# Masked attention layers: maxima split by the upper halves of their words, and the projections' bank read between exponential and seed

## The chip, the cores and the metric

One core of a Trainium2 chip runs the whole network as one program. The metric is the device time of one execution in microseconds; the kernel before takes 3803.99 us (median of 3 runs, 3799.57 to 3808.73).

## The reference

Four transformer layers on x (8 batches x 512 rows x 256), each with cross attention (16 heads of depth 16, keys and values from a context of 512 rows) and a feed-forward part. Layers 0, 1 and 3 use masked attention; layer 1 also adds an adjacency matrix and masks with minus infinity, so that a row whose keys are all masked becomes NaN:

```python
scores = jnp.einsum('bhqd,bhkd->bhqk', Q, K) / jnp.sqrt(jnp.float32(D))
scores = scores + adj[None, None, :, :]                            # layer 1 only
scores = jnp.where(mask == 0, jnp.float32(-jnp.inf), scores)
weights = jax.nn.softmax(scores, axis=-1)
out = jnp.einsum('bhqk,bhkd->bhqd', weights, V)                    # then @ Wo + bo
```

Layer 2 (relative attention) and the four feed-forward parts are not touched.

## The kernel before, in words

Each layer part is a stage of its own, with a barrier of all engines behind it. The function `masked_attention` (L48) is called for layers 0, 1 and 3. A batch is 16 steps (4 groups of 4 heads, each with 4 blocks of 128 keys); a step has two half steps, called positions p = 0 to 31, each for two heads. Every engine runs its own list, in order, over these positions; semaphores tie them together. Batches 1 to 4 run in a loop of two rounds of two batches.

Scores are made twice. First the max units (`pe_max_unit`, L261): queries on partitions, 7 steps ahead; DVE adds the bias and reduces to the negated row maximum in one instruction (L460) into `nmax`. There are four max units to a step, two PSUM banks for them, and each unit waits until DVE has read the one two before it. Then the scores proper (`pe_scores`, L276), with keys on partitions, which need the maximum as three further rows of the contraction. Their bank `p2_ps[half]` is first filled with the turned bias: by ACT, the "seed" (`act_seed`, L512), or by two matmuls with the identity (L281). Function `by_act` decides: in layer 1 ACT seeds both half steps, in layers 0 and 3 only half 0. ACT takes the exponential of the bank (L529), and PE multiplies by the values (L292). ACT seeds the bank for step s+1 right behind the exponential of step s.

To bring the maxima into the contraction, DVE splits them at positions 2, 10, 18 and 26 (`dve_split_maxima`): copy to bf16 (L405), remainder (L408), copy to bf16 (L411), remainder (L414), each waiting for the one before, and placed between and behind the position's two reductions. The last one raises `m_split`. At the next position (3, 11, 19, 27) PE turns the parts into rows (`pe_maxima`, L251) in the shared bank `front_ps`, ACT copies these to `m_row` (L490), and SP issues four DMAs into the query stack. In layer 1 the split at position 26 is joined by `dve_all_masked`, three DVE instructions (L420, L422, L424) that make the NaN rows from `nmax`.

The bank `front_ps` is shared by all side work of a batch: values at positions 0 and 4, the output projection at 8 and 12 (both read by DVE), turned input at 14 and 16, key projection at 20 and 22, query projection at 24 and 28 (read by ACT in `act_shared`, L484 and L497), and the four maxima. PE makes a projection in two pieces around the position's second max unit; it waits for the read of the bank's use before. ACT reads the bank at the start of the position behind, so behind the seed. POOL (`pool_frame`) splits queries and keys, makes the mask biases, and adds the output bias to the residual in one instruction (L546).

Of the kernel before, what the change touches and what calls it, by code (L numbers as in the profile page):

```python
# [14 lines left out]
P = 128  # L15
# [32 lines left out]
def masked_attention(nc, x_sb, ident, ident_bf, ctxT_dram, w, layer, mask, maskT, adj=None, adjT=None):  # L48
# [15 lines left out]
    with ctx:  # L64
        def sb(name, shape, dt):
            return ctx.enter_context(nc.sbuf_tensor(f + name, shape, dt))
# [26 lines left out]
        heads_out = sb("heads_out", [P, S], F32)  # L93
        heads_outT = sb("heads_outT", [P, DC, S], F32)
        rsum = sb("rsum", [P, BLOCKS, 1], F32)
        nmax = sb("nmax", [P, 2, TPB, GH], F32)
        m_rest = sb("m_rest", [P, TPB, GH], F32)
        m_parts = sb("m_parts", [P, TPB, GH, 3], BF16)
        m_row = sb("m_row", [GH * 3, 2, S], BF16)
        ones_row = sb("ones_row", [3, S], BF16)  # L100
        stats = sb("stats", [P, TPB, 6], F32)
# [145 lines left out]
        def pe_maxima(pe, n, j, base, b):  # L247
            pe.wait_ge(front_read, base + n)
            pe.wait_ge(m_split, b * NG + j + 1)
            for t in range(TPB):  # L250
                last = nc.tensor.matmul(front_ps[0:GH * 3, t * P:(t + 1) * P],  # L251
                                        m_parts[:, t, :, :].rearrange("p h k -> p (h k)"), ident_bf[:, :],
                                        start=True, stop=True)
            last.then_inc(front_full, 1)

# [138 lines left out]
                nc.vector.tensor_tensor(tiles, front_ps[:, :].rearrange("p (a n) -> p a n", a=2), tiles,  # L394
                                        ALU.add).then_inc(front_read, 1)

        def dve_split_maxima(dve, b, j, step):

            G = b * NG + j
            if step == 0:  # L400
                dve.wait_ge(maxed, (G + 1) * GH * TPB)
                if later(G):

                    dve.wait_ge(m_row_ready, G)
                nc.vector.tensor_copy(m_parts[:, :, :, 0], nmax[:, j % 2, :, :]).then_inc(m_step, 1)  # L405
            elif step == 1:
                dve.wait_ge(m_step, G * 3 + 1)
                nc.vector.tensor_tensor(m_rest[:, :, :], nmax[:, j % 2, :, :], m_parts[:, :, :, 0], ALU.subtract).then_inc(m_step, 1)  # L408
            elif step == 2:
                dve.wait_ge(m_step, G * 3 + 2)  # L410
                nc.vector.tensor_copy(m_parts[:, :, :, 1], m_rest[:, :, :]).then_inc(m_step, 1)  # L411
            else:
                dve.wait_ge(m_step, G * 3 + 3)
                nc.vector.tensor_tensor(m_parts[:, :, :, 2], m_rest[:, :, :], m_parts[:, :, :, 1], ALU.subtract).then_inc(m_split, 1)  # L414

        def dve_all_masked(dve, b, par):

            k = b * 3
            nan = nan_rows[:, par, :]
            nc.vector.tensor_scalar(nan, nmax[:, 0, :, 0], 1e29, 3e38, ALU.is_gt, ALU.mult).then_inc(nan_step, 1)  # L420
            dve.wait_ge(nan_step, k + 1)
            nc.vector.tensor_scalar(nan, nan, 3e38, 0.0, ALU.mult, ALU.mult).then_inc(nan_step, 1)  # L422
            dve.wait_ge(nan_step, k + 2)
            nc.vector.tensor_scalar(nan, nan, 0.0, None, ALU.add).then_inc(nan_step, 1)  # L424

        def dve_split_first(dve, which, i):

# [10 lines left out]
        def dve_positions(dve, b, par, positions, plan):  # L438
            for p in positions:
                s, half = p // 2, p % 2  # L440
                pair = (2 * half, 2 * half + 1)
                split = group_split(b, p)
                a, over, j, t = ahead(s)
                for n, kind, i in shared(plan, p, 1):
                    dve_shared(dve, n, kind, i, uses_before(b), b, par)
                if split is not None:
                    dve_split_maxima(dve, b, split, 0)
                if has(b, a) and half == 0:
                    if every_mask and j == 0:
                        dve.wait_ge(bias_ready, (b + over) * MK + t + 1)  # L450
                    G = b * NG + a // TPB
                    if t == 0 and later(G - 1):
                        dve.wait_ge(m_split, G - 1)
                for i in pair:
                    if has(b, a):
                        unit = (b * STEPS + a) * GH + i
                        if later(unit - NX + 1):
                            dve.wait_ge(maxed, unit - NX + 1)
                        dve.wait_ge(p1_done, unit + 1).then_inc(apart_dve, 1)
                        nc.vector.tensor_tensor_reduce(  # L460
                            out=sums[:, i % NX, :], in0=p1_ps[i % 2][:, :], in1=bias[:, t, :],
                            scale=-1.0, scalar=3.4028235e38, op0=ALU.add, op1=ALU.min,
                            accum_out=nmax[:, a // TPB % 2, t, i:i + 1]).then_inc(maxed, 1)
                    if split is not None:
                        if i == pair[0] and adj is not None and split % NG == 0:
                            dve_all_masked(dve, b + split // NG, (par + split // NG) % 2)
                        dve_split_maxima(dve, b, split, i % 2 + 1)
                if split is not None:
                    dve_split_maxima(dve, b, split, 3)
                j = (p - HEADS) // 8  # L470
                if (p - HEADS) % 8 < 4 and has(b, j * TPB):
                    dve_heads(dve, b, j, (p - HEADS) % 8)
                if has(b + 2, 0) and p == 7 and not opening(b):
                    dve_norm_input(dve, b + 2)
                if has(b + 2, 0) and p == 9:
                    dve_apply_norm(dve, b + 2)
# [37 lines left out]
        def act_positions(act, b, par, positions, plan):  # L514
            for p in positions:
                s, half = p // 2, p % 2
                for n, kind, i in shared(plan, p, 1):
                    act_shared(act, n, kind, i, uses_before(b), b, par)
                if p % 8 == 2 and has(b, s - 2):
                    G = b * NG + (s - 2) // TPB  # L520
                    act.wait_ge(pv_done, (G + 1) * TPB * GH)
                    if later(G):
                        act.wait_ge(o_turned, G)
                    nc.scalar.activation(oT_sb[:, :], oT_ps[:, :], ACT.Copy).then_inc(oT_read, 1)
                if has(b, s):
                    if later(b * STEPS + s - 1):
                        act.wait_ge(pv_done, (b * STEPS + s - 1) * GH)
                    act.wait_ge(p2_done, b * HALVES + p + 1).then_inc(apart_act, 1)
                    nc.scalar.activation(probs[:, s % 2 * 2 + half, :, :], p2_ps[half][:, :, :], ACT.Exp).then_inc(exp_done, 1)  # L529
                over, t = (s + 1) // STEPS, (s + 1) % STEPS  # L530
                if has(b, s + 1) and by_act(t, half):
                    act_seed(act, b, over, t, half)
# [8 lines left out]

        def pool_residual(pool, bn):
            pool.wait_ge(xn_ready, bn + 1)
            tile = x_sb[:, bass.ds(bn * TPB, TPB), :]
            bo = bo_bc[:, :].rearrange("p (a n) -> p a n", a=1).to_broadcast([P, TPB, D])
            nc.gpsimd.tensor_tensor(tile, tile, bo, ALU.add).then_inc(residual_biased, 1)  # L546

        def pool_split(pool, bn, which, i):

# [31 lines left out]
        def pool_frame(pool, b, par):  # L581

            after, then = has(b, 0) and has(b + 1, 0), has(b + 2, 0)
            for s in range(STEPS):
                if s == 0 and every_mask and has(b, 0) and later(b):
                    pool_mask(pool, b, MK - 1)
                if s in (1, 2) and after:
                    pool_split(pool, b + 1, 0, s - 1)
                if s == 3 and has(b + 1, 0):
                    pool_residual(pool, b + 1)  # L590
                if s == 4 and then and not opening(b):
                    pool_norm(pool, b + 2)
# [2323 lines left out]
```

## Time and profile before

| what | value |
|---|---|
| median of 3 runs | 3803.99 us |
| profiled execution, its span | 3814.43 us, 3812.7 us |
| masked layer 0, layer 1, layer 3 (start to next stage's start) | 16.1 to 672.2, 942.6 to 1673.1, 2754.0 to 3403.2 us |
| mean granted TensorE clock | 0.91 |
| PE, DVE, ACT, POOL busy share | 83%, 66%, 59%, 29% |

The stage starts are those of each stage's first POOL instruction. The three masked layers take 656.1, 730.5 and 649.2 us, together 2035.8 us, over half of the span. The busy share of an engine is a mean over stages with different limits. In rows of the timeline the first column is the start, the second the duration; in brackets stands the engine's idle time ahead of the instruction and who ended it. A matmul's duration is modelled and overlaps the next one's.

### The profile page before, as it was taken

What the parts mean: (1) busy time and instruction counts of PE and PEld (TensorE: products, weight loads), DVE (VectorE), ACT (ScalarE), POOL (GpSimd) and SP (SyncE); (2) the same over time, 40 slices, a digit from 0 to 9 for tenths busy, and PEclk for the clock granted to TensorE, in tenths of its full rate; (3) what the DMA queues carried; (4) which work ended last, traced back from release to release, by engine and by line L of the source; (5) the groups of instructions that cost most, each with busy time, mean ns of one, the idle gap of its engine ahead of it and who ended that gap; (6) DMA issues with size and microseconds to landing.
All of it is one profiled execution on the core that took longest, in us unless ns stands there. A gap on an engine that the chain in (4) does not pass through costs nothing. (4 is left out here: it accounts for less than half of the span.)

```text
span 3812.7 us, 67413 instructions
## 1 busy us (share of the span) xinstructions
PE 3150.8 (83%) x17142; PEld 1603.2 (42%) x17249; DVE 2502.5 (66%) x7668; ACT 2250.3 (59%) x3026; POOL 1117.3 (29%) x1194
## 2 busy tenths in 40 slices
PE   5999998787788888849977888888279999965997
PEld 3343432343333333216644555555134344324565
DVE  4777776787676677743225777878867787755431
ACT  1777777664388888951116666676547777750111
POOL 4344441000454555201114333331332221100332
PEclk8999999898799899969988999999589999985899
DMA  5322320000433334110028999997031221102332
GB/s 147 87 71 69 96 72 13 23 0 31 123 96 95 84 95 112 51 52 1 0 55 291 293 289 292 296 321 257 24 82 41 58 63 40 35 29 94 77 101 67
DMA packets 212155, 392.88 MB, mean 103 GB/s; under 512 B 24633, under 2 KB 76985, under 8 KB 211657
## 3 DMA queue, kind: packets, MB, share of 16 engines
q1 hardware_dynamic: 168777, 296.38, 28.1%
q10 hardware_dynamic: 36864, 83.90, 5.9%
q0 software_dynamic: 6144, 8.39, 1.3%
q8 instruction: 143, 2.34, 0.3%
q14 instruction: 227, 1.86, 0.2%
HBM read 189.88 MB, written 96.47 MB: 75 GB/s over the span
## 5 line engine op out<-in xcount | busy, mean ns | idle before, releaser
L460 DVE CUSTOM_DVE_ANT_0 A_sums<-A_p_ps,A_bias 128x512 bf16<-128x512 f32 x1536 | 1039.3, 688 | 434.0 <-PE A_p_ps L261 392.7
L529 ACT ACTIVATE A_probs<-A_p_ps 128x1024 f32<-128x1024 f32 x768 | 780.6, 1018 | 281.3 <-PE A_p_ps L276 186.2
L261 PE MATMUL A_p_ps<-A_k_stack,A_q_stack 96*128 96x512 bf16 x1536 | 604.0, 396 | 116.4 <-DVE A_nmax L460 109.8
L512 ACT ACTIVATE A_p_ps<-A_biasT 128x1024 f32<-128x1024 bf16 (+1 forms) x512 | 526.1, 1028 | 62.1 <-ACT A_probs L529 2.4
L276 PE MATMUL A_p_ps<-A_q_stack,A_k_stack 99*128 99x512 bf16 x1536 | 471.5, 389 | 39.0 <-ACT A_p_ps L512 34.4
L292 PE MATMUL A_oT_ps<-A_probs,A_v_aug 128*17 128x512 f32 x3072 | 419.1, 618 | 0.7 <-ACT A_probs L529 0.7
L261 PEld LDWEIGHTS A_p_ps<-A_k_stack,A_q_stack 96*128 96x128 bf16 x1536 | 149.7, 97 | 630.5 <-DVE A_nmax L460 539.7
L1100 DVE CUSTOM_DVE_ANT_0 A_scores<-A_qk_ps,A_rel_in 128x384 f32<-128x384 f32 (+3 forms) x512 | 232.5, 486 | 84.3 <-PE A_qk_ps L984 76.3
L1007 PE MATMUL A_t_ps<-ident,A_scores 128*128 128x128 f32 x1280 | 227.7, 299 | 61.4 <-DVE A_probsT L1090 52.6
L1155 ACT ACTIVATE A_rel_out<-A_rel_ps 128x1024 f32<-128x1024 f32 (+3 forms) x256 | 179.9, 703 | 144.0 <-PE A_rel_ps L973 142.4
L1090 DVE COPY A_probsT<-A_t_ps 128x384 f32<-128x384 f32 (+3 forms) x512 | 229.1, 485 | 54.1 <-PE A_t_ps L1007 46.4
L1162 ACT ACTIVATE A_scores<-A_scores,A_nmax 128x384 f32<-128x384 f32 (+3 forms) x512 | 257.4, 555 | 7.3 <-DVE A_nmax L1100 7.2
L276 PEld LDWEIGHTS A_p_ps<-A_q_stack,A_k_stack 99*128 99x128 bf16 x1536 | 144.1, 100 | 180.5 <-ACT A_p_ps L512 73.3
L1182 POOL TENSOR_SCALAR_AFFINE_SELECT A_rel_in<-A_rel_in 128x256 f32<-128x256 f32 x256 | 102.6, 409 | 397.3 <-DMA A_rel_in<-A_rel_dram 393.4
L1007 PEld LDWEIGHTS A_t_ps<-ident,A_scores 128*128 128x128 f32 x1280 | 151.8, 149 | 138.1 <-issue 56.4
L574 POOL TENSOR_SCALAR A_bias<-A_mask_in 128x512 bf16<-128x512 int32 (+2 forms) x68 | 131.5, 1934 | 209.0 <-DVE A_nmax L460 187.9
L574 POOL TENSOR_SCALAR A_biasT<-A_mask_in 128x512 bf16<-128x512 int32 (+2 forms) x68 | 131.9, 1940 | 136.9 <-PE A_p_ps L281 70.3
L2786 ACT ACTIVATE M_hid<-M_h_ps,M_b 128x512 f32<-128x512 f32 x64 | 44.0, 687 | 189.2 <-PE M_h_ps L2588 186.7
L555 POOL CAST A_parts<-A_qk 128x512 bf16<-128x512 f32 x84 | 51.2, 609 | 334.6 <-ACT A_qk L497 334.2
L2105 ACT ACTIVATE U_hid<-U_h_ps,U_hid_bias 128x512 f32<-128x512 f32 x64 | 44.0, 687 | 176.0 <-PE U_h_ps L1943 175.9
L984 PE MATMUL A_qk_ps<-A_k_stack,A_q_stack 96*128 96x384 bf16 (+3 forms) x512 | 127.2, 313 | 12.6 <-DVE A_nmax L1100 11.1
L281 PE MATMUL A_p_ps<-A_biasT,ident_bf 128*128 128x512 bf16 x420 | 132.6, 379 | 5.2
(345 smaller groups left out, 5452.2 us busy)
## 6 DMA issues: line engine op xcount, KB each, us to landing
A_k_stack<-A_parts SPq DMA_DIRECT2D x192, 256.0 KB, 5.0
A_q_stack<-A_parts SPq DMA_DIRECT2D x192, 256.0 KB, 5.5
A_rel_dram<-A_rel_out ACTq DMA_DIRECT2D x64, 512.0 KB, 5.0
A_rel_in<-A_rel_dram SPq DMA_DIRECT2D x64, 512.0 KB, 5.7
A_rel_dram<-A_rel_out ACTq DMA_DIRECT2D x64, 384.0 KB, 4.8
A_rel_in<-A_rel_dram SPq DMA_DIRECT2D x64, 384.0 KB, 5.3
A_ctxT<-in_ctxT SPq DMA_DIRECT2D x32, 512.0 KB, 6.4
A_mask_in<-in_mask SPq DMA_DIRECT2D x64, 256.0 KB, 4.5
```

The source lines that it names most:

```text
L261: nc.tensor.matmul(p1_ps[i % 2][:, :], q_stack[0:KS, a_par, j * GH + i, t * P:(t + 1) * P], k_stack[0:KS, a_par, j * GH + i, :], start=Tru ...
L276: last = nc.tensor.matmul(p2_ps[half][:, i % 2, :], k_stack[:, par, j * GH + i, kb * P:(kb + 1) * P], q_stack[:, par, j * GH + i, :], star ...
L292: nc.tensor.matmul(oT_ps[CW * i:CW * i + HD + 1, :], v_aug[:, v_par, kb, j * GH + i, :], probs[:, (s - 1) % 2 * 2 + i // 2, i % 2, :], sta ...
L460: nc.vector.tensor_tensor_reduce(out=sums[:, i % NX, :], in0=p1_ps[i % 2][:, :], in1=bias[:, t, :], scale=-1.0, scalar=3.4028235e38, op0=A ...
L512: nc.scalar.activation(p2_ps[half][:, :, :], turned, ACT.Copy).then_inc(seeded, 1)
L529: nc.scalar.activation(probs[:, s % 2 * 2 + half, :, :], p2_ps[half][:, :, :], ACT.Exp).then_inc(exp_done, 1)
L574: last = nc.gpsimd.tensor_scalar(dst, mask_in[:, k % 2, :], 0.0, NEG, ALU.is_equal, ALU.mult)
L1007: last = nc.tensor.transpose(t_ps[:, i, kb, :], scores[(p - TURN_LAG) % NP][:, i, kb * P:(kb + 1) * P], ident[:, :])
L1090: nc.vector.tensor_copy(probsT[u % NP][:, i, 0:nk, :], t_ps[:, i, 0:nk, :]).then_inc(copied, 1)
L1100: nc.vector.tensor_tensor_reduce(out=scores[p % NP][:, i, 0:n], in0=qk_ps[i][:, 0:n], in1=rel_in[s % NI][:, (2 * half + i) * n:(2 * half + ...
L1155: nc.scalar.activation(rel_out[a % NO][:, 2 * half * n:(2 * half + 2) * n].rearrange("p (i n) -> p i n", i=2), rel_ps[:, :, 0:n], ACT.Copy ...
L1162: nc.scalar.activation(scores[u % NP][:, i, 0:n], scores[u % NP][:, i, 0:n], ACT.Exp, bias=nmax[:, u % NP, i:i + 1], scale=-1.0).then_inc( ...
```

## The change

The maxima lie in a new tile `maxima` [P, 2, TPB, 3, GH] of f32. The reduction writes part 0. The bf16 part that PE uses is not a copy but the upper half of each f32 word, seen through a bitcast with a stride of two; two subtractions on DVE make the parts 1 and 2. The maxima's rows in `m_row` are ordered part by part, so that SP's four DMAs read partitions with a stride of 4. DVE's guard for a new group waits for `m_row_ready` in place of `m_split`. The NaN rows are made by POOL at step 14. POOL's residual bias is four instructions of 128x256 in place of one of 128x1024. ACT reads the shared bank in the same position: behind its exponential and ahead of its seed.

```diff
-        nmax = sb("nmax", [P, 2, TPB, GH], F32)
-        m_rest = sb("m_rest", [P, TPB, GH], F32)
-        m_parts = sb("m_parts", [P, TPB, GH, 3], BF16)
+        maxima = sb("maxima", [P, 2, TPB, 3, GH], F32)
+        maxima_high = maxima[:, :, :, :, :].rearrange("p a t k h -> p (a t k h)").bitcast(BF16)[:, 1::2].rearrange(
+            "p (a t k h) -> p a t k h", a=2, t=TPB, k=3)
...
-        def dve_split_maxima(dve, b, j, step):
+        def dve_split_maxima(dve, b, j, k):
...
+            whole, high = maxima[:, j % 2, :, k, :], maxima_high[:, j % 2, :, k, :]
+            if k == 0:
                 dve.wait_ge(maxed, (G + 1) * GH * TPB)
...
+                dve.wait_ge(m_step, G + 1)
+            nc.vector.tensor_tensor(maxima[:, j % 2, :, k + 1, :], whole, high,
+                                    ALU.subtract).then_inc((m_step, m_split)[k], 1)
...
                     if t == 0 and later(G - 1):
-                        dve.wait_ge(m_split, G - 1)
+                        dve.wait_ge(m_row_ready, G - 1)
+                    if t == 0 and adj is not None and a // TPB % NG == 2:
+                        dve.wait_ge(nan_step, (b + over) * 3 + 1)
...
-                    if split is not None:
-                        if i == pair[0] and adj is not None and split % NG == 0:
-                            dve_all_masked(dve, b + split // NG, (par + split // NG) % 2)
-                        dve_split_maxima(dve, b, split, i % 2 + 1)
-                if split is not None:
-                    dve_split_maxima(dve, b, split, 3)
+                    if split is not None and i == pair[0]:
+                        dve_split_maxima(dve, b, split, 1)
...
         def act_positions(act, b, par, positions, plan):
             for p in positions:
                 s, half = p // 2, p % 2
-                for n, kind, i in shared(plan, p, 1):
-                    act_shared(act, n, kind, i, uses_before(b), b, par)
...
                     nc.scalar.activation(probs[:, s % 2 * 2 + half, :, :], p2_ps[half][:, :, :], ACT.Exp).then_inc(exp_done, 1)
+                for n, kind, i in shared(plan, p):
+                    act_shared(act, n, kind, i, uses_before(b), b, par)
                 over, t = (s + 1) // STEPS, (s + 1) % STEPS
                 if has(b, s + 1) and by_act(t, half):
                     act_seed(act, b, over, t, half)
...
+            for t in range(TPB):
+                tile = x_sb[:, bass.ds(bn * TPB + t, 1), :].rearrange("p a n -> p (a n)")
+                last = nc.gpsimd.tensor_tensor(tile, tile, bo_bc[:, :], ALU.add)
+            last.then_inc(residual_biased, 1)
+
+        def pool_all_masked(pool, bn, par):
+
+            k, nan = bn * 3, nan_rows[:, par, :]
+            pool.wait_ge(m_split, bn * NG + 1).then_inc(apart_pool, 1)
+            if later(bn - 1):
+                pool.wait_ge(front_read, use_of(bn - 1, "out", 1) + 1).then_inc(apart_pool, 1)
+            nc.gpsimd.tensor_scalar(nan, maxima[:, 0, :, 0, 0], 1e29, 3e38, ALU.is_gt, ALU.mult).then_inc(nan_step, 1)
...
+                if s == 14 and adj is not None and has(b + 1, 0):
+                    pool_all_masked(pool, b + 1, 1 - par)
...
-                             m_row[3 * h:3 * h + 3, j % 2, :]).then_inc(m_placed[j % 2], 16)
+                             m_row[h:GH * 3:GH, j % 2, :]).then_inc(m_placed[j % 2], 16)
```

## Rows read from the trace of the kernel before

**Rows 1.** Page, costliest groups: ACT's exponentials and seeds.
```profile
L529 ACT ACTIVATE A_probs<-A_p_ps 128x1024 f32<-128x1024 f32 x768 | 780.6, 1018 | 281.3 <-PE A_p_ps L276 186.2
L512 ACT ACTIVATE A_p_ps<-A_biasT 128x1024 f32<-128x1024 bf16 (+1 forms) x512 | 526.1, 1028 | 62.1 <-ACT A_probs L529 2.4
```

**Rows 2.** Busy (count) of PE, PEld, DVE, ACT, POOL by window; clock; DMA; GB/s.
```profile
1416.93:1499.38 82.45, 69.89 (x345) 28.69 (x345) 59.99 (x182) 71.31 (x80) 43.43 (x36) 0.94 0.36 97
396.00:470.00 74.00, 69.68 (x370) 30.08 (x375) 56.96 (x177) 55.78 (x63) 33.10 (x27) 1.00 0.32 80
```

**Rows 3.** Idle before L251 in layer 1, by releaser: us, times.
```profile
  DVE A_m_parts L414: 51.3, 34
```

**Rows 4.** Waits in layer 1: us in total, times, longest.
```profile
PE A_front_ps L230 <- ACT A_m_row L490: 8.1, 6, 2.1
```

**Rows 5.** ACT's waits in layer 1 from 1043.5 to 1661 us.
```profile
ACT A_probs L529 <- PE A_p_ps L276: 31.5, 44, 2.7
ACT A_qk L497 <- PE A_front_ps L230: 7.4, 8, 1.6
```

**Rows 6.** Timeline of DVE, layer 1, a split at position 26.
```profile
1416.79 1.23 DVE L420 TENSOR_SCALAR A_nan_rows<-A_nmax 128x4 f32<-128x4 f32 x1
...
1418.26 0.52 DVE L424 TENSOR_SCALAR A_nan_rows<-A_nan_rows 128x4 f32<-128x4 f32 x1
...
1420.14 0.19 DVE L414 TENSOR_TENSOR A_m_parts<-A_m_rest,A_m_parts 128x16 bf16<-128x16 f32 x1
```

**Rows 7.** Timeline of POOL at that time.
```profile
1416.73 1.26 POOL L578 TENSOR_TENSOR A_biasT<-A_biasT,A_adj_in 128x512 f32<-128x512 f32 x1
```

**Rows 8.** Timeline of PE at that time.
```profile
1420.38 0.39 PE L251 MATMUL A_front_ps<-ident_bf,A_m_parts 128*12 128x128 bf16 x4 [2.63 <-DVE A_m_parts L414]
```

**Rows 9.** Timeline of ACT behind that split.
```profile
1423.60 1.02 ACT L529 ACTIVATE A_probs<-A_p_ps 128x1024 f32<-128x1024 f32 x1 [1.44 <-PE A_p_ps L276]
...
1426.56 0.69 ACT L497 ACTIVATE A_qk<-A_front_ps,A_bq 128x512 f32<-128x512 f32 x1 [0.79 <-PE A_front_ps L230]
```

**Rows 10.** Timeline of ACT behind a split at position 2, layer 1.
```profile
1278.49 1.02 ACT L529 ACTIVATE A_probs<-A_p_ps 128x1024 f32<-128x1024 f32 x1 [1.94 <-PE A_p_ps L276]
```

**Rows 11.** Another of the same, and a key read at position 20.
```profile
1487.02 0.69 ACT L497 ACTIVATE A_qk<-A_front_ps,A_bk 128x512 f32<-128x512 f32 x1 [1.60 <-PE A_front_ps L230]
...
1527.86 1.02 ACT L529 ACTIVATE A_probs<-A_p_ps 128x1024 f32<-128x1024 f32 x1 [0.65 <-PE A_p_ps L276]
```

**Rows 12.** Timeline of PE and ACT, layer 1, key projection at position 22.
```profile
1408.07 1.03 PE L230 MATMUL A_front_ps<-A_ctxT,A_wk 128*128 128x256 f32 x4
...
1407.43 1.01 ACT L529 ACTIVATE A_probs<-A_p_ps 128x1024 f32<-128x1024 f32 x1
...
1409.51 0.67 ACT L497 ACTIVATE A_qk<-A_front_ps,A_bk 128x512 f32<-128x512 f32 x1
```

**Rows 13.** Timeline of PE and ACT, layer 0, key projection at position 20.
```profile
431.77 1.03 PE L230 MATMUL A_front_ps<-A_ctxT,A_wk 128*128 128x256 f32 x4
...
435.24 0.60 PE L276 MATMUL A_p_ps<-A_q_stack,A_k_stack 99*128 99x512 bf16 x2
...
430.97 1.02 ACT L529 ACTIVATE A_probs<-A_p_ps 128x1024 f32<-128x1024 f32 x1 [0.59 <-PE A_p_ps L276]
...
433.08 0.67 ACT L497 ACTIVATE A_qk<-A_front_ps,A_bk 128x512 f32<-128x512 f32 x1
```

**Rows 14.** Idle before L251 by releaser, in layer 0 and then in layer 3.
```profile
  DVE A_m_parts L414: 10.9, 22
...
  DVE A_m_parts L414: 12.4, 23
```

**Rows 15.** Timeline of all engines, layer 1, a split beside POOL's residual.
```profile
1271.55 2.35 POOL L546 TENSOR_TENSOR x_sb<-x_sb,A_bo_bc 128x1024 f32 x1
1271.66 2.28 DVE L414 TENSOR_TENSOR A_m_parts<-A_m_rest,A_m_parts 128x16 bf16<-128x16 f32 x1
```

**Rows 16.** Line L405: duration in ns, shortest, median, longest.
```profile
L405 DVE CAST A_m_parts<-A_nmax x96: 174/183/2035, 69.3 to 3369.8; 128x16 bf16<-128x16 f32 x96
```

More of the change, by code:

```diff
@@ L251, in pe_maxima @@
                 last = nc.tensor.matmul(front_ps[0:GH * 3, t * P:(t + 1) * P],
-                                        m_parts[:, t, :, :].rearrange("p h k -> p (h k)"), ident_bf[:, :],
+                                        maxima_high[:, j % 2, t, :, :].rearrange("p k h -> p (k h)"), ident_bf[:, :],
                                         start=True, stop=True)
@@ L395, in dve_shared @@
                                         ALU.add).then_inc(front_read, 1)
-        def dve_split_maxima(dve, b, j, step):
+        def dve_split_maxima(dve, b, j, k):
             G = b * NG + j
-            if step == 0:
+            whole, high = maxima[:, j % 2, :, k, :], maxima_high[:, j % 2, :, k, :]
+            if k == 0:
                 dve.wait_ge(maxed, (G + 1) * GH * TPB)
[L402 to L411, printed above, removed]
-            else:
[L413 to L424, printed above, removed]
+            else:
+                dve.wait_ge(m_step, G + 1)
+            nc.vector.tensor_tensor(maxima[:, j % 2, :, k + 1, :], whole, high,
+                                    ALU.subtract).then_inc((m_step, m_split)[k], 1)
         def dve_split_first(dve, which, i):
@@ L462, in dve_positions @@
                             scale=-1.0, scalar=3.4028235e38, op0=ALU.add, op1=ALU.min,
-                            accum_out=nmax[:, a // TPB % 2, t, i:i + 1]).then_inc(maxed, 1)
-                    if split is not None:
-                        if i == pair[0] and adj is not None and split % NG == 0:
-                            dve_all_masked(dve, b + split // NG, (par + split // NG) % 2)
-                        dve_split_maxima(dve, b, split, i % 2 + 1)
-                if split is not None:
-                    dve_split_maxima(dve, b, split, 3)
+                            accum_out=maxima[:, a // TPB % 2, t, 0, i:i + 1]).then_inc(maxed, 1)
+                    if split is not None and i == pair[0]:
+                        dve_split_maxima(dve, b, split, 1)
                 j = (p - HEADS) // 8
@@ L543, in pool_residual @@
             pool.wait_ge(xn_ready, bn + 1)
-            tile = x_sb[:, bass.ds(bn * TPB, TPB), :]
-            bo = bo_bc[:, :].rearrange("p (a n) -> p a n", a=1).to_broadcast([P, TPB, D])
-            nc.gpsimd.tensor_tensor(tile, tile, bo, ALU.add).then_inc(residual_biased, 1)
+            for t in range(TPB):
[8 more added lines that the diff above has]
+            nc.gpsimd.tensor_scalar(nan, maxima[:, 0, :, 0, 0], 1e29, 3e38, ALU.is_gt, ALU.mult).then_inc(nan_step, 1)
+            pool.wait_ge(nan_step, k + 1).then_inc(apart_pool, 1)
+            nc.gpsimd.tensor_scalar(nan, nan, 3e38, 0.0, ALU.mult, ALU.mult).then_inc(nan_step, 1)
+            pool.wait_ge(nan_step, k + 2).then_inc(apart_pool, 1)
+            nc.gpsimd.tensor_scalar(nan, nan, 0.0, None, ALU.add).then_inc(nan_step, 1)
         def pool_split(pool, bn, which, i):
```

## The prediction

> **What bounds the kernel now.** I read the page's costliest groups first, then one batch of each masked layer by window, then the waits, then the timeline around the splits. The reader is to see two different limits.
>
> In layers 0 and 3 it is PE. A batch takes 74.0 us, and PE is busy for 69.7 of them; ACT has 55.8, DVE 57.0 [rows 2]. What PE loses there is lost for good; what ACT or DVE gain is not seen.
>
> In layer 1 ACT seeds both half steps. Exponentials and seeds take 1018 and 1028 ns each [rows 1]; back to back a pair takes some 2.1 us, so 32 pairs make 67 of a batch's 82.5 us. With the bank reads and the copies of the outputs (some 0.5 us each, fourteen) ACT is at about 75. Its busy share by window, 71.3 of 82.5 us, is the union of overlapping rows; PE has 69.9 [rows 2]. So ACT is the bound, and time is lost where ACT itself stands: 31.5 us for scores and 7.4 us for a projection from 1043.5 to 1661 us [rows 5], 38.9 in all. PE's own waits matter only as far as they come back as such idle time.
>
> **The split of the maxima.** Before: four DVE instructions of about 0.18 us in a group, and the last comes behind the position's second reduction. After: two, the second behind the first reduction. Some 0.36 us of DVE work goes, and `m_split` comes earlier by that and by one reduction (0.69 us or a little less). What counts is PE at L251. In layer 1 it stood for the last remainder (L414) 51.3 us in 34 waits [rows 3]. These are of two kinds.
>
> At position 26 the NaN rows are made between the two reductions. L420 starts at 1416.79 and L424 ends at 1418.78, so 1.99 us; the split ends at 1420.33 [rows 6]. PE had stood 2.63 us when its transposes began [rows 8], so it was ready at 1417.75. ACT then stood 1.44 us before an exponential and 0.79 before the projection behind it [rows 9], 2.23 us in all. Without the NaN work and the two last instructions the second subtraction would start at about 1416.8, where L420 did. But POOL has an instruction from 1416.73 to 1417.99 [rows 7], and L420 took 1.23 us on four elements a partition, to just POOL's end. The same is seen where L414 took 2.28 us beside POOL's 2.35 us residual and ended with it [rows 15]. I take the subtraction to be held likewise, to 1418.2: PE still stands 0.4 us, and 1.8 us of ACT's 2.23 come back. The split comes eight times; I count six (in the others ACT doesn't stand behind it): 11 us.
>
> The Trainium skill, "GPSIMD Engine Reference", section Key points, says that GpSimd shares its SBUF interfaces with VectorE and contends with instructions in a two-port mode or with two SBUF inputs. That speaks against this change, as both instructions left have two SBUF inputs; the trace agrees for L414. By that rule the saving at position 26 is 1.8 us, as taken; without it, 2.2.
>
> At position 2 ACT stood 1.94 us behind the split beside the residual [rows 10], and 0.65 us in a common case [rows 11]. There are six such, from 0.5 to 2.5 us with what follows. The residual in four pieces of a quarter (2.35/4, so 0.6 us) holds DVE for at most 0.6 us instead of 2.28. One us each: 6 us.
>
> In layers 0 and 3 the idle ahead of L251 for L414 is 10.9 and 12.4 us [rows 14]. This counts the weight loads' queue too, which stands without harm while matmuls run, so half is an upper guess: 5 us each, which takes in one copy in layer 0 that POOL held for 2.04 us [rows 16]. Together 10; the bounds are 0 and 23.3.
>
> **The read of the bank, maxima.** Layer 1 only (half 1 has no seed in layers 0 and 3, so nothing changes there). The read goes ahead of a seed of 1.03 us. PE stood 8.1 us for it before the key and query projections [rows 4]; ACT paid with waits such as 1.60 us before a key read [rows 11]. Of ACT's 7.4 us [rows 5] some 4 don't follow a NaN split; I take 3. The seed behind it is later by the read, 0.6 us, and PE then has a projection to do first, so nobody waits. Bounds 0 and 4.4.
>
> **The read of the bank, projections.** This is the cost. Before, ACT seeded while PE finished the projection; now ACT stands behind its exponential until the bank is full. In layer 1 the exponential ends at 1408.44 and the projection at 1409.10 [rows 12]: 0.66 us. But a delayed ACT finds PE further ahead at the next read, so in a run of three reads it is paid once: 0.7 us in each of six batches with projections, 4.2 us. Turned input (positions 14, 16) is short and ready in time. In layer 0 the exponential ends at 431.99, the projection at 432.80 [rows 13]: ACT stands 0.81 us. The read (issued 0.15 later, 0.6 long) and the seed (1.03) then end at about 434.6; PE's scores that need the seed start at 435.24 [rows 13]. Cover of 0.6 us, so nothing is lost; if it were gone, each read would cost up to 0.81.
>
> **The rest.** DVE's guard on `m_row_ready` is for the group before the last, long read: 0. POOL's three tiny instructions (the fastest such row on DVE is 0.17 us; POOL, some 0.3 each) sit between bias builds; DVE needs the first only three steps later, and ACT's seeds need the mask build behind it over 5 us later: 0, at most 1 us a batch. SP issues the same four DMAs per group, of three rows each, and the scores need them four positions later: 0. PE's weights with a stride of two: 12 columns, 0; bounds 0 to 0.1 us for each of 96 groups. Strided operands on DVE, 16 elements: the same, either sign.
>
> **Sum.** Layer 1: 11 + 6 + 3 - 4.2, about 16 us. Layers 0 and 3: 10. Together 26 us less. The profiled execution took 3814.4 us around its span of 3812.7, so 3788; it lies 10.4 above the median of 3804.0, so the median becomes 3778.
>
> **Rivals.**
> A, larger: ACT's waits in layer 1 go altogether (38.9 us) and the full 23.3 of layers 0 and 3 return: 62 us less, 3742. For it: ACT is the bound and all its releasers are PE. Against: the largest waits near position 10 stem from DVE's norm, which stays.
> B, hidden: PE's waits vanish and come back as waits for seeds or for POOL-held subtractions, so the change doesn't bring `m_split` forward where it matters. Left are the NaN instructions and little else, about 5 us: 3799. For it: two-input instructions are held by POOL [rows 7, 15], and the reads make seeds later.
> C, slower: the stand between exponential and seed. It decides from the point where PE's next scores already wait for the seed, a cover of 0.6 us in layers 0 and 3. Price: 24 reads in each, 48 x 0.81 = 39 us, and 24 x 0.66 = 16 in layer 1, less the 26 + 4 gained elsewhere: 25 slower, 3829. For it: the seeds are late by 1.5 us in every such position. Against: ACT stands idle for 18 of 74 us there.
>
> **How the numbers follow.** About 0.2%, 8 us, is what a measurement of this kernel can tell from no change. Forecast 0.56 (own range 3760 to 3792), A 0.12, B 0.20, C 0.12. B lies at the edge, so a quarter of it counts as faster: faster 0.73, same 0.15, slower 0.12. For eight in ten I go from 3748, near A, to 3803, past B; C is left out.
>
> **What would show it.** Right: in layer 1, L251's idle for the split falls from 51 to under 15 us; a batch takes 80 us instead of 82.5; ACT's rows show a stand of 0.3 to 0.8 us before L497 directly behind an exponential; POOL's residual rows are 0.6 us. In layers 0 and 3 a batch takes 73.3 to 74 us, and L276 doesn't wait for L512 more than now. Wrong: PE's scores in layers 0 and 3 wait for seeds behind every key or query read; the two subtractions are often over 1 us; layer 1's batch stays at 82 us though L251 no longer waits.

## The result

The changed kernel takes 3746.17 us (median of 4 runs, 3740.91 to 3750.79) against 3806.36 us of the kernel before in the same runs: ratio 0.9842, interval 0.9818 to 0.9865, 60 us less. Run once more, beside other runs of the kernel before, it came to 0.9859 (0.9841 to 0.9877). The prediction was 3778, 26 us less, where 60 came. The measured time lies 2 us below the low end of the range (3748).

The title names the bank reads of the projections only. The change moves all of ACT's bank reads between exponential and seed, the maxima's too, and that one turns out to be the part that pays.

The profiled execution has a span of 3744.7 us. By stage, from the first POOL instruction of each:

| stage, us | before | after | predicted difference |
|---|---|---|---|
| masked layer 0 | 656.1 | 647.8 | -5 |
| masked layer 1 | 730.5 | 686.3 | -16 |
| masked layer 3 | 649.2 | 645.2 | -5 |
| the five untouched stages | 1760.8 | 1749.4 | 0 |

The untouched stages differ by 11 us with the same code; over all kernels of this study layer 2's attention took between 707 and 717 us, whatever was changed. So a single profile's stages carry some 5 us of scatter each. The two profiles differ by 68 us (that of the kernel before is of an execution 8 us above the median), the medians by 60. A quieter measure is used below: in layer 1 the time from the first copy of the outputs' bank (L524 before, L502 after) to the 29th, 28 groups or seven batches. In the changed kernel these are the two rows (timeline of ACT; start, duration):

```profile
1021.89 0.58 ACT L502 ACTIVATE A_oT_sb<-A_oT_ps 128x512 f32<-128x512 f32 x1
...
1554.20 0.58 ACT L502 ACTIVATE A_oT_sb<-A_oT_ps 128x512 f32<-128x512 f32 x1
```

So 532.3 us; before it was 568.4 (from 1043.49 to 1611.92). That is 36 of the layer's 44 us. The second profile of the changed kernel gave 528.8. Layers 0 and 3 over the same 28 groups: 512.7 to 505.7 and 510.5 to 507.0.

The page's groups that answer to [rows 1], ACT's exponentials and seeds (busy, mean ns, idle before):

```profile
L507 ACT ACTIVATE A_probs<-A_p_ps 128x1024 f32<-128x1024 f32 x768 | 780.4, 1017 | 220.6 <-PE A_p_ps L276 148.2
L492 ACT ACTIVATE A_p_ps<-A_biasT 128x1024 f32<-128x1024 bf16 (+1 forms) x512 | 525.8, 1027 | 52.3 <-ACT A_m_row L470 7.5
```

The work is the same, the exponentials' idle time fell by 61 us. One batch by window, columns as in [rows 2]:

```profile
1360.00:1435.00 75.00, 66.31 (x344) 26.26 (x342) 55.46 (x168) 69.47 (x78) 43.90 (x41) 0.98 0.39 106
380.00:453.00 73.00, 69.41 (x375) 29.88 (x374) 55.01 (x167) 54.92 (x62) 33.20 (x30) 1.00 0.31 79
```

In these windows layer 1's batch went from 82.5 to 75 us (mean of the seven batches: 81.2 to 76.0) and ACT is busy for 69.5 of them, 93%. PE does the same work in 66.3 instead of 69.9 us, at a granted clock of 0.98 instead of 0.94 of full speed. Over the whole 28 groups, before and after:

```profile
1043.49:1611.92 568.43, 476.60 (x2345) 184.91 (x2345) 414.03 (x1241) 495.29 (x542) 283.94 (x224) 0.94 0.33 89
1021.89:1554.20 532.31, 462.04 (x2344) 176.86 (x2344) 388.02 (x1161) 487.82 (x542) 291.11 (x263) 0.97 0.35 95
```

In these stretches the granted clock is either 1.00 or 0.50 of full speed. From the means 0.94 and 0.97 some 70 us at half speed can be worked out before and some 30 after, and PE is busy 14.6 us less with the same work. One such stretch of before: PE stood 2.63 us at L251 until 1420.38 [rows 8], and from 1421.90 to 1425.30 the granted clock is 0.50. PE's shorter time can be a part of why ACT waits less for it; how large a part, no run separates. What L251 waits for in layer 1, as in [rows 3]:

```profile
  issue: 13.4, 29
  DVE A_maxima L405: 1.3, 3
```

51.3 us became 1.3 (of the 51.3, 28.1 stood on PE's matmul queue and 23.2 on the weight loads'). [rows 5] cover a longer stretch than 28 groups, so here are ACT's waits over the 28 groups alone, before:

```profile
ACT A_probs L529 <- PE A_p_ps L276: 30.2, 41, 2.7
ACT A_qk L497 <- PE A_front_ps L230: 7.4, 8, 1.6
ACT A_probs L529 <- issue: 3.8, 1, 3.8
ACT A_probs L529 <- ACT A_m_row L490: 3.7, 12, 0.4
```

and after:

```profile
ACT A_probs L507 <- PE A_p_ps L276: 15.2, 19, 3.6
ACT A_p_ps L492 <- ACT A_m_row L470: 6.9, 28, 0.3
ACT A_qk L477 <- PE A_front_ps L230: 1.7, 8, 0.3
```

Of 37.6 us for PE 16.9 are left. With the waits that name another releaser or none (one wait of 3.6 to 3.8 us is given to PE in one profile and to "issue" in another) the idle time in rows fell by 22 us, of a gain of 36. The other 14 are not idle time in any row. They are in the distances between ACT's instructions. Before, with the maxima read behind the seed (timeline of ACT, kernel before):

```profile
1419.50 1.01 ACT L529 ACTIVATE A_probs<-A_p_ps 128x1024 f32<-128x1024 f32 x1
1420.62 1.03 ACT L512 ACTIVATE A_p_ps<-A_biasT 128x1024 f32<-128x1024 f32 x1
1421.59 0.57 ACT L490 ACTIVATE A_m_row<-A_front_ps 12x512 bf16<-12x512 f32 x1
```

and after:

```profile
1373.38 1.01 ACT L507 ACTIVATE A_probs<-A_p_ps 128x1024 f32<-128x1024 f32 x1
1374.29 0.57 ACT L470 ACTIVATE A_m_row<-A_front_ps 12x512 bf16<-12x512 f32 x1
1375.14 1.03 ACT L492 ACTIVATE A_p_ps<-A_biasT 128x1024 f32<-128x1024 f32 x1 [0.28 <-ACT A_m_row L470]
1376.10 1.01 ACT L507 ACTIVATE A_probs<-A_p_ps 128x1024 f32<-128x1024 f32 x1
1377.27 0.69 ACT L477 ACTIVATE A_qk<-A_front_ps,A_bq 128x512 f32<-128x512 f32 x1 [0.17 <-PE A_front_ps L230]
1377.86 1.02 ACT L492 ACTIVATE A_p_ps<-A_biasT 128x1024 f32<-128x1024 f32 x1
```

The seed starts 1.12 us behind its exponential, since it overwrites the bank and waits for that one's end. The bank read doesn't wait: it starts 0.91 behind. So a read in this place costs 0.22 us less than behind the seed. From the exponential to the next one, in steps with a read of the maxima, it took 3.05 us before (median, with 0.22 or 0.39 of wait for the read's own end) and takes 2.72 after. With turned input it is 2.58 and 2.33, with a projection 2.70 and 2.58. The 28 groups hold 28, 12 and 24 such steps: by these medians 9, 3 and 3 us, together some 15. This distance from start to start is called the pitch below.

### The profile page after: what moved, and what is told of

The parts are those of the page before. It is cut to its first block and busy times, and to the rows that moved or that the text cites. A ratio compares the mean times of both kernels' runs of the same rounds, so it can differ in the third digit from the quotient of the medians.

```text
span 3744.7 us, 67361 instructions
## 1 busy us (share of the span) xinstructions
PE 3126.9 (84%) x17249; PEld 1590.8 (42%) x17249; DVE 2445.0 (65%) x7452; ACT 2234.1 (60%) x3026; POOL 1133.9 (30%) x1290
## 5 line engine op out<-in xcount | busy, mean ns | idle before, releaser
L276 PEld LDWEIGHTS A_p_ps<-A_q_stack,A_k_stack 99*128 99x128 bf16 x1536 | 141.4, 99 | 183.9 <-ACT A_p_ps L492 81.2
L281 PE MATMUL A_p_ps<-A_biasT,ident_bf 128*128 128x512 bf16 x512 | 152.6, 378 | 0.0
```

Source lines behind the costliest of these rows:

```text
L276: last = nc.tensor.matmul(p2_ps[half][:, i % 2, :], k_stack[:, par, j * GH + i, kb * P:(kb + 1) * P], q_stack[:, par, j * GH + i, :], star ...
```

## The experiments

All times are medians against runs of the kernel before on the same chip. "28 groups" is the stretch of layer 1 told above, one profiled execution each; two of the changed kernel differ by 3.5 us, so only differences well over that are read. "Early" means between exponential and seed, "late" behind the seed.

| kernel | median us | ratio, interval | 28 groups us |
|---|---|---|---|
| before | 3804 to 3812 | 1 | 568.4 |
| changed | 3746.17; 3753.81 | 0.9842 (0.9818, 0.9865); 0.9859 (0.9841, 0.9877) | 532.3; 528.8 |
| changed, all reads late | 3791.92 | 0.9953 (0.9936, 0.9970) | 561.3 |
| before, all reads early | 3790.03 | 0.9955 (0.9937, 0.9973) | 550.3 |
| before, NaN rows on POOL | 3809.97 | 1.0006 (0.9989, 1.0023) | 564.1 |
| before, new split | 3798.28 | 0.9972 (0.9955, 0.9989) | 571.9 |
| changed, only maxima early | 3763.04 | 0.9888 (0.9866, 0.9911) | 531.8 |
| changed, only projections early | 3791.47 | 0.9955 (0.9942, 0.9968) | 567.1 |
| changed, outputs' copy early too | 3745.56 | 0.9823 (0.9800, 0.9846) | 524.2 |
| changed, NaN rows on DVE | 3749.28 | 0.9863 (0.9837, 0.9890) | 531.2 |
| before, split and maxima early | 3766.13 | 0.9882 (0.9863, 0.9901) | 539.4 |
| before, maxima early | 3788.07 | 0.9944 (0.9924, 0.9965) | 551.9 |
| changed, filler ahead of each seed | 3755.49 | 0.9863 (0.9847, 0.9879) | 530.7 |
| changed, residual in one piece | 3753.52 | 0.9852 (0.9832, 0.9873) | 532.2 |
| changed, outputs early, row signal late | 3744.16 | 0.9829 (0.9810, 0.9847) | 523.2 |

**Each part by itself.** First the reads put back in the changed kernel:

```diff
             for p in positions:
                 s, half = p // 2, p % 2
+                for n, kind, i in shared(plan, p, 1):
+                    act_shared(act, n, kind, i, uses_before(b), b, par)
...
-                for n, kind, i in shared(plan, p):
-                    act_shared(act, n, kind, i, uses_before(b), b, par)
                 over, t = (s + 1) // STEPS, (s + 1) % STEPS
```

> The changed kernel with one part undone: ACT reads the shared bank again at the start of the next position, behind the seed. Theory 1 (order): in the trace of after a seed starts 1.13 us behind its exponential, since it waits for that exponential's end, while a bank read starts 0.91 behind it and the seed 0.48 (input, 0.59 projection) behind the read; so a read in between costs 0.22 us less, 36 such in layer 1, and for the maxima 2.72 against 3.05 us, 30 such: 16 to 18 us in layer 1, so this kernel takes about 3764 us and its layer 1 some 703 us instead of 686. Theory 2 (the prediction's): the reads ahead of the seed cost ACT 4 us, the maxima's read gives 3, so this kernel stays at 3746 plus or minus 3.

Measured 3791.92, far slower than either theory said: all other parts together are worth 7 us of the 36 in 28 groups, and 0.5% in all. The prediction's count for the reads (3 gained, 4 lost) is refuted. Then the same edit the other way round, on the kernel before:

> The kernel before with this one part of the change: ACT reads the shared bank between exponential and seed. Theory 1 (order): layer 1 gains 16 us or a little more, 3788 us; layers 0 and 3 nothing. Theory 2 (the prediction's): gain 3, cost 4, so 3806 plus or minus 3. Rival C of the prediction: slower, up to 3829, with PE's scores waiting for seeds in layers 0 and 3.

3790.03 and 18 us in 28 groups, as the pitch would have it; layer 0's stage took 656.1 us as before and 28 groups of layers 0 and 3 took 512.7 and 509.6 us against 512.7 and 510.5, so rival C is refuted too. But 18 and 7 make 25, not 36.

The NaN rows alone:

```diff
-                        if i == pair[0] and adj is not None and split % NG == 0:
-                            dve_all_masked(dve, b + split // NG, (par + split // NG) % 2)
...
+                if s == 14 and adj is not None and has(b + 1, 0):
+                    pool_all_masked(pool, b + 1, 1 - par)
```

> The kernel before with this one part: the NaN rows are made by POOL at step 14. Prediction's way of counting: ACT's idle behind the split at position 26 is 2.2 us in each of six batches, most of it from the NaN work of 1.99 us, so 10 us less, 3796. If PE's wait of 2.6 us comes back in full in all eight batches: 18 us less, 3788. Layers 0 and 3 unchanged.

Nothing that the medians show, and 4 us in 28 groups, which is within the scatter. PE's stand at position 26, 1.3 to 2.6 us in the eight splits before, fell to 0.5 to 1.3 us, but that was not worth the 11 us of the sum. And the split alone (with the new order of the rows in `m_row` and DVE's guard, which belong to it):

```diff
-                nc.vector.tensor_copy(m_parts[:, :, :, 0], nmax[:, j % 2, :, :]).then_inc(m_step, 1)
...
+            nc.vector.tensor_tensor(maxima[:, j % 2, :, k + 1, :], whole, high,
+                                    ALU.subtract).then_inc((m_step, m_split)[k], 1)
```

> The kernel before with this one part: the maxima split by the upper halves of their words, two subtractions, NaN rows still on DVE, reads late, residual in one piece. Prediction's way: layers 0 and 3 gain 4 to 5 us each, layer 1 some 6: 3791. If only the stands seen on PE's matmul queue count (2.6 and 3.8 us in layers 0 and 3): 3794. In layer 1 the idle of L251 for the split falls by the two last instructions and one reduction, about 1 us at positions 2 and 26.

9 us less in all, and none of it in layer 1's 28 groups (571.9). PE's waits from 929 us to the end of layer 1 show where it went (us in total, times, longest):

```profile
PE A_front_ps L230 <- ACT A_m_row L480: 13.5, 11, 2.1
PE A_front_ps L235 <- ACT A_m_row L480: 10.4, 6, 2.0
PE A_front_ps L251 <- DVE A_maxima L405: 8.0, 7, 1.2
PE A_front_ps L242 <- ACT A_m_row L480: 3.6, 2, 2.0
```

At L251 PE stands 8 us instead of 28.1 on its matmul queue, and 27.5 us instead of 14.5 (8.1 at L230, 3.4 at L235, 3.0 at L242) for ACT's read of the maxima before the next projection. Much of the stand has moved one step on.

**Which reads.** Only the maxima's read early, with the rest of the change:

```diff
+                for n, kind, i in shared(plan, p, 1):
+                    if not (kind == "m"):
+                        act_shared(act, n, kind, i, uses_before(b), b, par)
...
                 for n, kind, i in shared(plan, p):
-                    act_shared(act, n, kind, i, uses_before(b), b, par)
+                    if (kind == "m"):
+                        act_shared(act, n, kind, i, uses_before(b), b, par)
```

> The changed kernel, but only the maxima's read stays between exponential and seed; the six reads of projections and turned input per batch go back behind the seed. So far in layer 1, over 28 groups in the middle of the layer: before 568.5 us, reads early alone 550.2, all but the reads 561.3, the whole change 532.3. So 11 us come only when both are there. Theory I (maxima chain): an early m_split is worth nothing while the maxima's read stands behind a seed of 1 us, and PE's next projection waits for that read; then this kernel keeps the interaction and loses only the pitch of 36 reads x 0.22 = 8 us less the 5 us ACT stands for the bank: about 3750. Theory II (ACT is just full): the interaction comes from ACT's shorter work as such, whichever reads; then half of all is lost: about 3765.

28 groups 531.8, all of the gain. The reads of projections and turned input are worth nothing there that can be seen; that their pitch and ACT's stand for the bank cancel is the likely reading. The median is 17 us above the changed kernel's first one and 9 above its second; whether a few us of that are real is not settled. The reverse, with the condition turned round:

> The reverse: projections and turned input are read between exponential and seed, the maxima's read goes back behind the seed. Theory I (maxima chain): the interaction of 11 us goes, and 30 x 0.33 = 10 us of pitch, so about 21 to 30 us over the changed kernel: 3770 to 3776. Theory II: about half of the reads' part, 3760.

567.1, close to the 568.4 of the kernel before: without the maxima's read all the rest of the change is worth 1 us in layer 1, and 7 where the projections' reads are late too (561.3). So with the maxima late, the projections' early reads cost some 6 us, in one profile each. PE's waits in it from 929 us to the end of layer 1:

```profile
PE A_front_ps L230 <- ACT A_m_row L470: 22.6, 12, 2.1
PE A_front_ps L235 <- ACT A_m_row L470: 11.0, 6, 2.0
PE A_front_ps L242 <- ACT A_m_row L470: 3.2, 2, 1.6
```

36.8 us, against these in the changed kernel (929 to 1616 us; L242's row there is under 1):

```profile
PE A_front_ps L230 <- ACT A_m_row L470: 9.8, 12, 0.9
PE A_front_ps L235 <- ACT A_m_row L470: 3.9, 6, 0.8
```

With `m_split` early the read is ready to go, but it stands in ACT's list behind a seed of 1 us; PE's next projection waits for it, and ACT's read of that projection, or the scores behind it, then wait for PE. ACT's largest waits in this kernel, over its 28 groups, show the way back:

```profile
ACT A_probs L510 <- PE A_p_ps L276: 23.9, 32, 2.4
ACT A_qk L477 <- PE A_front_ps L230: 19.1, 13, 2.8
```

43.0 us for PE, where the changed kernel has 16.9. It is a loop through both engines.

**Does it need the NaN rows on POOL?** In the changed kernel they go back to DVE, between the two reductions:

```diff
                     if split is not None and i == pair[0]:
+                        if adj is not None and split % NG == 0:
+                            dve_all_masked(dve, b + split // NG, (par + split // NG) % 2)
                         dve_split_maxima(dve, b, split, 1)
```

> The changed kernel with the NaN rows back on DVE, between the two reductions at position 26. Alone on the kernel before, moving them gave nothing that the medians show (1.0006 [0.9989, 1.0023]) and 4.5 us in 28 groups of layer 1. Theory I (maxima chain): with the read early the 2 us of DVE work are now on the chain eight times: 12 to 16 us over the changed kernel, 3760. Rival: ACT's or DVE's slack hides it here too: 3746 to 3750.

531.2 and 3749: the rival, they are hidden here too. Next the smallest pair, on the kernel before: the new split and the maxima's read, nothing else (the two edits shown above).

> The kernel before with two parts only: the split by upper halves, and the maxima's read (alone) between exponential and seed. NaN rows on DVE, residual in one piece, projections read late. Chain theory: these two are the whole gain; 28 groups of layer 1 take 532 us plus or minus 4, layers 0 and 3 as in the changed kernel, so 3750 to 3760. Rival: what is missing (NaN rows on POOL, residual in pieces) works only together; then 545 us or more and over 3770.

Between the two: 539.4, that is 29 of the 36 us. And the maxima's read without the split:

> The kernel before with one part: the maxima's read between exponential and seed, the old split of four instructions. Chain theory: the read early shortens the chain by a seed, the late split (25 us of stand at L251 in 28 groups) stays: between 568 and 532, about 550 us as with all reads early, 3788. Rival: the read alone does it all, 532 to 538.

551.9: 16 us by itself, at an unchanged granted clock (0.94 over the 28 groups, as before), so this part of the gain doesn't come through the clock. So over 28 groups the split is worth -3 (slower, within the scatter) with the read late, and 12 with it early.

**The changed kernel again,** as the reference on that chip:

> The changed kernel itself once more, on the chip of the next three, as their reference. Expected at its first ratio, 0.984, so some 60 us under the kernel before, with 532 us over 28 groups of layer 1. If the kernel with only the maxima read early (0.9888 in the last call, yet 531.8 us over the same groups) is really slower, this one must be clearly below 0.989; if that was the scatter between executions, the two meet.

0.9859, clearly below 0.9888 only by the middle values; the intervals (0.9841 to 0.9877, 0.9866 to 0.9911) touch. So it stays open as said.

**The residual in one piece,** for the 8 us between 539.4 and 531.8:

```diff
+            tile = x_sb[:, bass.ds(bn * TPB, TPB), :]
+            bo = bo_bc[:, :].rearrange("p (a n) -> p a n", a=1).to_broadcast([P, TPB, D])
+            nc.gpsimd.tensor_tensor(tile, tile, bo, ALU.add).then_inc(residual_biased, 1)
```

> The changed kernel with POOL's residual back in one instruction of 2.35 us. Between the kernel with split and maxima's read alone (539.4 us over 28 groups of layer 1) and the one with the NaN rows on POOL and the residual in four pieces (531.8) lie 8 us, and the NaN rows back on DVE changed nothing (531.2). Residual theory: this kernel takes 537 to 540 us there, and a DVE instruction of the split is again seen with 1 us or more beside the residual; 3758. Rival: NaN rows and residual cover for each other, either alone is enough; then 532 and 3750.

532.2: no effect in layer 1. In layer 0 one batch of seven took 80.6 us instead of 77.5, the one where a split meets the residual. So neither the NaN rows nor the residual, taken back singly, costs the 8 us. Both together do seem to: with the projections' reads late, the kernel that has both takes 531.8 us and the one that has neither 539.4; with all reads late it is 561.3 and 571.9. That they cover for each other fits this, but no run takes back exactly these two from the changed kernel.

**The pitch by itself.** An instruction without use ahead of every seed of layer 1:

```diff
         def act_seed(act, b, over, s, half):
+            if adj is not None:
+                n = seeds(b + over, s, half)
...
+                    act.wait_ge(filled, n - 1).then_inc(apart_act, 1)
+                    nc.scalar.activation(filler[:, :], bq_sb[:, 0:1], ACT.Copy).then_inc(filled, 1)
```

> The changed kernel with an extra instruction on ACT, 128 x 1 elements, ahead of every seed of layer 1 (256 in all). It does nothing for the result. Pitch theory: where no read stands there, ACT is idle 0.22 us until the exponential has ended, so the filler fits in: seed still 1.13 us behind the exponential, 190 fillers free, and only the 66 behind a read cost some 0.1 to 0.2 us each: 532 us become 540 at most, 3755. Rival: the 0.22 us are ACT's own cost to turn from one instruction to the next; then each filler adds its 0.2 us, 45 us in 28 groups, 3795.

530.7 and 3755.49 beside 528.8 and 3753.81 of the changed kernel on the same chip, where 224 fillers of 0.20 us in the 28 groups would be 45 us. 160 of them stand directly behind an exponential, and there they cost nothing. The 28 behind the maxima's read do lengthen their step, from 2.72 to 2.92 us (medians), some 6 us in all; in the total that doesn't show. In its timeline the seed still starts 1.13 us behind the exponential, with the filler in between:

```profile
1179.65 1.02 ACT L516 ACTIVATE A_probs<-A_p_ps 128x1024 f32<-128x1024 f32 x1
1180.55 0.20 ACT L488 ACTIVATE A_filler<-A_bq 128x1 f32<-128x1 f32 x1
1180.78 1.03 ACT L501 ACTIVATE A_p_ps<-A_biasT 128x1024 f32<-128x1024 f32 x1
```

So the 0.22 us are a real gap, which other work fills, and not ACT's own cost of turning from one instruction to the next.

**Going on in that direction.** The copy of the outputs' bank put into the same gap, in layer 1:

```diff
-                if p % 8 == 2 and has(b, s - 2):
...
+                if adj is not None:
+                    act_outputs(act, b, s, p)
                 for n, kind, i in shared(plan, p):
                     act_shared(act, n, kind, i, uses_before(b), b, par)
```

> The changed kernel, and in layer 1 the copy of the outputs' bank (once in a group, at the first half of its second step) also goes between exponential and seed. Theory of the pitch: a seed starts 1.13 us behind its exponential because it waits for that one's end, anything else 0.91 behind it, so each copy saves 0.22 us: 31 x 0.22 = 6.8 us where ACT is the bound, so 3740. Rival: the copy comes a microsecond later, PE's first product of the next group waits for it, and the time stays at 3746 or rises by up to 10.

524.2: 8 us less than the first profile of the changed kernel and 4.6 less than the second, 6.8 expected. The step with the copy takes 2.33 instead of 2.57 us (median of 27), so the pitch is as expected. The ratio, 0.9823, can't be told from the changed kernel's. Then the signal for the maxima's rows behind the seed as well:

```diff
                 if has(b, s + 1) and by_act(t, half):
                     act_seed(act, b, over, t, half)
+                for n, kind, i in shared(plan, p):
+                    if kind == "m" and adj is not None:
+                        act.wait_ge(front_read, uses_before(b) + n + 1).then_inc(m_row_ready, 1)
```

> The changed kernel with two more moves on ACT in layer 1: the outputs' copy between exponential and seed (measured before: 524.2 against 532.3 and 528.8 us over 28 groups), and the wait for the maxima's read, which raises m_row_ready, put behind the seed instead of ahead of it. Pitch theory: the seed then starts 0.58 instead of 0.85 us behind the maxima's read, 28 x 0.27 = 7.5 us less: 516 to 518 us over 28 groups, 3736. Rival: the query stack's rows come a seed later, the scores of a new group wait for them or ACT only finds PE not ready: 524 us or more.

523.2, the rival's number. The seed does start 0.48 us behind the read instead of 0.85 (timeline of ACT):

```profile
1162.80 0.57 ACT L470 ACTIVATE A_m_row<-A_front_ps 12x512 bf16<-12x512 f32 x1
1163.28 1.00 ACT L493 ACTIVATE A_p_ps<-A_biasT 128x1024 f32<-128x1024 f32 x1
```

but what ACT wins it now waits away for PE, over the same 28 groups:

```profile
ACT A_probs L512 <- PE A_p_ps L276: 17.8, 23, 4.5
ACT A_qk L478 <- PE A_front_ps L230: 6.7, 12, 0.7
```

24.5 us for PE, where the kernel with only the outputs' copy moved has these:

```profile
ACT A_probs L511 <- PE A_p_ps L276: 13.4, 20, 4.5
ACT A_p_ps L492 <- ACT A_m_row L470: 6.9, 28, 0.3
ACT A_qk L477 <- PE A_front_ps L230: 2.6, 9, 0.9
```

The 6.9 us for ACT's own read went, and 8.5 came for PE. So at this point a shorter ACT list alone no longer shortens layer 1. With 0.9829 (0.9810 to 0.9847) this kernel is the fastest median of the study, 3744 us, but not shown to beat the changed one.

## Why the prediction was wrong

**The bounds: right.** PE in layers 0 and 3, ACT in layer 1. Layer 1's batch went close to ACT's own time of 75 us, as counted (76.0 on the mean of seven; 80 was forecast).

**"The read of the bank, maxima" is the step that failed.** It took 3 us with bounds 0 and 4.4. Alone it gave 16 us in 28 groups, and with the rest of the change 35 (567.1 against 532.3). Two things were missing. It counted only waits that stood in rows, ACT's for a projection and PE's for the read, and the 0.22 us between an exponential and its seed stand in no row of waits; 30 reads at 0.33 us make 10. And it read the wait for the maxima's read, 8.1 us [rows 4] (14.5 with the two other lines that wait for it), as the size of that limit, when it was only what was left of it behind the larger stand at L251: with the split early and the read late it is 27.5.

**What the sum left out altogether is the pitch.** For ACT's waits the sum had 11 + 6 + 3 = 20 us in layer 1, and those for PE fell by 21 in 28 groups. That these two agree is luck: the 17 us booked on split, NaN rows and residual gave 7 us (561.3) as long as the reads were late, and the rest came only together with the maxima's read. Beside it the sum had 4.2 us of loss for the early reads, and the runs show some 15 us of gain in the pitch of the 64 steps with a read.

**"The split of the maxima", 11 and 6 us in layer 1: nothing by itself.** 1.8 of ACT's 2.23 us were to come back at position 26. With the split alone PE stands for the read instead, and with the NaN rows moved alone the medians don't move (the residual's 6 us were never moved alone). As terms of a sum they were wrong in kind: the two waits follow each other in one loop, so the terms don't add. The first removed is worth 0, the second 16, both 29.

**The NaN rows: not needed by themselves.** Back on DVE in the changed kernel they cost nothing (531.2 against 532.3 and 528.8) with the residual in pieces.

**POOL holding the subtraction: right, and harmless.** In the changed kernel one subtraction lasts just as long as POOL's instruction beside it (timelines of DVE and POOL):

```profile
1387.90 1.15 DVE L405 TENSOR_TENSOR A_maxima<-A_maxima 128x16 f32<-128x16 f32 x1
...
1387.86 1.15 POOL L554 TENSOR_TENSOR A_parts<-A_qk,A_parts 128x512 bf16<-128x512 f32 x1
```

The rule of the Trainium skill cited for it ("GPSIMD Engine Reference", Key points) agrees with this trace for an instruction with two SBUF inputs. Instructions with one input were held too: L420 for 1.23 us [rows 6, 7], a copy at L405 for 2.04 us [rows 16]; rival B named [rows 7] for two-input instructions, and L420 is none. Whether those two ran in a two-port mode, which the page names too, no view shows. With these holds L251 still stood only 1.3 us for DVE. The residual's pieces take 0.73 us each, not 0.6.

**"The read of the bank, projections": the stand was about right, its pay was left out.** From the exponential to a projection's read 1.04 us pass (median of 24) where 0.91 is the shortest: some 3 us over 28 groups, near the 4.2 counted. The step as a whole got shorter by 0.12 us, which the prediction didn't count. In layers 0 and 3 the cover held. Timeline of ACT in layer 0, changed kernel:

```profile
435.36 0.69 ACT L477 ACTIVATE A_qk<-A_front_ps,A_bq 128x512 f32<-128x512 f32 x1 [0.95 <-PE A_front_ps L230]
```

ACT stands 0.95 us there, and PE's wait for a seed in layer 0 is 1.7 us in 3 times, as before.

**Layers 0 and 3: right within the scatter.** 5 each predicted, 7.0 and 3.5 over 28 groups, and five other profiles whose kernels have the same code for these layers lie between 505.6 and 508.0. PE's own stand at L251 was 2.6 and 3.8 us on the matmul queue and is gone; some 3 of layer 0's 7 us lie in the one batch where a split met the residual (80.4 to 77.5 us).

**Rival A** came nearest in time (3742), in part by luck: it had all of ACT's waits in layer 1 go and no pitch, and 16.9 us of waits are left while the pitch gave some 15. It had 0.12. **Rival B**, waits that vanish and come back elsewhere, is what the split alone showed, behind the maxima's read and not behind seeds; with that read early it failed.

## What to carry to other kernels

Where engines pass work round in a loop, the waits in the trace are the last arrivals only: take one away and its time can turn up at the next semaphore, so price such edits together, or follow the chain to see what is late next and how late. On an engine that is the bound, look at the distance from start to start and not at idle time alone: an instruction that waits for the end of the one just ahead of it leaves a gap that no row of waits shows (0.22 us here), and independent work that fits into it was free here.

## What the runs showed that was not expected

The gap behind a 128x1024 exponential for an instruction that waits for its end is 0.22 us (1.13 against 0.91 from start to start), and a 0.20 us instruction fits in it without any cost (160 times in the 28 groups). Removing 2 us of DVE work on which PE stood 1.3 to 2.6 us, eight times in a layer, changed no median. A DVE instruction of 16 elements, 0.17 to 0.19 us alone, lasts as long as the POOL instruction beside it: 1.15 us beside 1.15, 2.28 beside 2.35.
